# Cross-attention and sparse feed-forward on one core: the gates move from a transposed mask to an addition in the accumulators, and the probabilities' second half gets two buffers

## The chip, the cores and the metric

The kernel runs on one core of a Trainium2 chip. Its time is device time in microseconds (us), from the first to the last instruction. The engines are TensorE (PE: matmuls; PEld: its weight loads), VectorE (DVE), ScalarE (ACT), GpSimd (POOL) and SyncE (SP, which issues most DMAs). Each has its own instruction stream, and they meet in semaphores.

## The reference, cut to what matters

16 batches of 100 tokens with 1024 features (x), and 361 context rows per batch. All weights and data are float32.

```python
x = x + xattn(layernorm(x), ctx)          # 32 query heads of 128, 4 key/value heads
# q = latents @ Wq; k, v = concat(ctx, latents) @ Wk, Wv      (461 keys)
# attn = softmax(q k^T / sqrt(128)); out = (attn @ v) @ Wo
x = x + ffn(layernorm(x))
def ffn(x):                               # 1600 tokens, 3584 inner features in 56 groups of 64
    inter = x @ c1_w.T @ c2_w.T           # rank 16
    idx = argmax of inter in each group of 64
    h = relu(x . w1[idx])                 # one inner feature of each group is open
    return h @ w2t[idx]
```

## The kernel before

Products of float32 values are made of three passes: each operand is split in a high part, rounded to the fast float32 format (F32R), and a low part, the rest, and high times high, high times low and low times high are added (`PAIRS`). ACT makes the high part by a copy, DVE or POOL the low part by a subtraction.

The stages follow one another, each in a block of its own that ends when all engines have ended: keys and values, queries, attention (1195 to 2006 us in the trace), output projection, normalisation, gate weights, hidden layer (2673 to 3214 us), down projection. The change touches two.

**Attention** (`attend`). The 800 query rows of a (batch, key/value head) pair, a *group* G, are 6 tiles of 128 rows and a rest of 32; the rests of the four groups of a batch make one more tile that comes first. So a batch has 25 tiles, in steps I. In each step PE does `score(I)` (3 matmuls of 128x462), then `weigh` for tiles long done (4 matmuls, probabilities times values), then `turn(I-3)` (4 transposes of the probabilities). DVE takes the negative maximum, ACT the exponential, DVE the reciprocal of the sum, POOL scales (L1239), PE turns, ACT copies the turned tile into `pt` (L1361), DVE writes its low part (L1409). `pt` holds a whole group, 800 columns: the first 384 are weighed as half h=0, the other 416 as h=1, each in three parts in three steps. The last 32 columns of h=1 come from the rests' tile, `pt_tail`: POOL brings them in with `bring_tail(G)` (L1227). That copy stands in POOL's stream where the loop of POOL is 4 steps past tile 3 of the group, that is in the step of tile 1 of the next group, behind the scaling and behind a part of `split_q` (L1196, L1200: POOL splits the next queries in steps 0 to 2 of each group), and it first waits until the group before was weighed whole, since `pt` is the only buffer. PE's `weigh(G, 1, 0)` waits for it (`tail_in`) at L1305.

**Hidden layer** (`hidden_layer`). 1344 of the 1600 tokens (the first 256 go another way, by gathered rows that DVE multiplies and sums: `dot`, L1546, six in a pair) times all 3584 inner features. The features come in 28 blocks j of 128, two to a pair i, p = j mod 2: the first pair is written out, twelve run in PE's and ACT's loop, the last is written out. For a block PE turns the weights (`turn_w`, 2x4 transposes into the two banks `turn`), ACT and DVE split them into `w[p]` (L1749, L1779), and PE sums four tiles of 336 tokens into four banks `hid_acc` (`sums`, 24 matmuls each). The gates of a pair, 13 tiles of 128 tokens by 256 features, come in four lots of 4, 4, 4 and 1 tiles (`gates`, L1679, then `pick` on DVE: maximum, equal, times key, maximum, and L1803, the mask with 1 at the open feature). The mask has tokens on its partitions, the sums have features there. So PE turns the mask with a bf16 identity (`turn_mask`, L1691, 11 transposes a block) into the banks `turn`, once both halves of the next block's weights have left them (the wait for `low` at L1733), ACT copies it to `mask_t` (L1758), and DVE evacuates each tile with one instruction, max(sum, 0) times mask (L1827), in between its picks and dots. The order on PE is that of `body` (L1702), on DVE of L1830.

```python
                    if another:
                        pe.wait_ge(low, 2 * j + 4)
                    turn_mask(i, m, p, 0)
```

## Time and profile before

| | |
|---|---|
| time, median of 3 runs | 3652.81 us (3650.86 to 3655.02) |
| profiled execution: time, span | 3654.5 us, 3652.8 us |
| mean granted TensorE clock | 0.977 of full |
| PE busy | 3448.0 us, 94% of the span |
| DVE busy | 2295.6 us, 63% |
| ACT busy | 1369.2 us, 37% |
| POOL busy | 881.1 us, 24% |

Busy time of PE is that of modelled matmuls: the end of one lies beyond the start of the next. So what PE really lost at a place is best read from starts: where the next group of instructions starts, against where it starts when nothing is waited for. The granted clock has two levels, full (2.4 GHz) and half (1.2 GHz).

### The profile page before, as it was taken

What the parts mean: (1) busy time and instruction counts of PE and PEld (TensorE: products, weight loads), DVE (VectorE), ACT (ScalarE), POOL (GpSimd) and SP (SyncE); (2) the same over time, 40 slices, a digit from 0 to 9 for tenths busy, and PEclk for the clock granted to TensorE, in tenths of its full rate; (3) what the DMA queues carried; (4) which work ended last, traced back from release to release, by engine and by line L of the source; (5) the groups of instructions that cost most, each with busy time, mean ns of one, the idle gap of its engine ahead of it and who ended that gap; (6) DMA issues with size and microseconds to landing.
All of it is one profiled execution on the core that took longest, in us unless ns stands there. A gap on an engine that the chain in (4) does not pass through costs nothing. (4 is left out here: it accounts for less than half of the span.)

```text
span 3652.8 us, 51935 instructions
## 1 busy us (share of the span) xinstructions
PE 3448.0 (94%) x18370; PEld 3060.2 (84%) x18370; DVE 2295.6 (63%) x3858; ACT 1369.2 (37%) x2560; POOL 881.1 (24%) x1100
## 2 busy tenths in 40 slices
PE   6999999799999999999999899999789999989999
PEld 5888888799999888888888688688589999977877
DVE  5555576777765677777776433433368888766775
ACT  3333344343432776777776322322411111121120
POOL 0000000000000766676665100000001111135443
PEclk8999999899999999999999899999889999999999
DMA  3333332454443333333332644644313444488886
GB/s 125 95 101 107 101 96 79 117 139 120 118 123 106 111 109 106 107 95 102 106 107 60 198 123 120 187 119 120 115 68 132 150 151 147 147 304 313 263 289 215
DMA packets 477859, 501.44 MB, mean 137 GB/s; under 512 B 172548, under 2 KB 372228, under 8 KB 477652
## 3 DMA queue, kind: packets, MB, share of 16 engines
q1 hardware_dynamic: 441988, 371.79, 34.3%
q0 software_dynamic: 34608, 124.90, 10.1%
q8 instruction: 117, 1.92, 0.2%
q10 hardware_dynamic: 1056, 2.10, 0.2%
q14 instruction: 90, 0.74, 0.1%
HBM read 383.68 MB, written 115.02 MB: 137 GB/s over the span
## 5 line engine op out<-in xcount | busy, mean ns | idle before, releaser
L2083 PE MATMUL wo_acc<-wo_w,wo_l 128*128 128x512 f32 (+1 forms) x2496 | 576.0, 393 | 23.3 <-DVE wo_l L2033 23.3
L427 PE MATMUL kv_bank<-kv_wo,kv_so 128*128 128x512 f32 x2436 | 574.1, 395 | 16.4 <-DVE kv_wo L519 11.0
L2083 PEld LDWEIGHTS wo_acc<-wo_w,wo_l 128*128 128x128 f32 (+1 forms) x2496 | 462.5, 186 | 136.6 <-DVE wo_w L2057 25.3
L427 PEld LDWEIGHTS kv_bank<-kv_wo,kv_so 128*128 128x128 f32 x2436 | 457.6, 190 | 110.9 <-issue 17.4
L815 PE MATMUL pr_bank<-pr_xo,pr_wp 128*128 128x400 f32 x2688 | 498.8, 347 | 28.9 <-ACT pr_s L882 13.4
L815 PEld LDWEIGHTS pr_bank<-pr_xo,pr_wp 128*128 128x128 f32 x2688 | 493.6, 190 | 31.7 <-DVE pr_wp L899 24.0
L26 PE MATMUL hid_acc<-x1t,hid_w 128*128 128x336 f32 x2688 | 442.6, 323 | 1.4 <-DVE c_raw L1827 0.9
L2352 PE MATMUL w_acc<-w_w,w_l 128*128 128x512 f32 (+1 forms) x1848 | 422.0, 391 | 12.1 <-DVE w_l L2291 12.1
L26 PEld LDWEIGHTS hid_acc<-x1t,hid_w 128*128 128x128 f32 x2688 | 426.4, 194 | 2.1 <-issue 1.1
L2352 PEld LDWEIGHTS w_acc<-w_w,w_l 128*128 128x128 f32 (+1 forms) x1848 | 339.5, 184 | 94.4 <-DVE w_l L2291 12.3
L1311 PE MATMUL outs<-pt,v 128*128 128x384 f32 (+3 forms) x1536 | 347.1, 348 | 28.6 <-issue 14.4
L1409 DVE TENSOR_TENSOR pt<-turned,pt 128x512 fp32r<-128x512 f32 x384 | 264.0, 688 | 156.9 <-ACT pt L1361 153.8
L2033 DVE TENSOR_TENSOR wo_l<-wo_l_raw,wo_l 128x512 fp32r<-128x512 f32 (+1 forms) x208 | 139.3, 672 | 343.3 <-ACT wo_l L2006 343.3
L26 PE MATMUL scores<-kt,q_parts 128*128 128x462 f32 x1152 | 338.2, 402 | 3.9 <-ACT probs L1367 3.9
L1311 PEld LDWEIGHTS outs<-pt,v 128*128 128x128 f32 (+1 forms) x1536 | 277.4, 188 | 66.6 <-issue 30.7
L1239 POOL TENSOR_SCALAR probs<-probs,inverse 128x461 f32<-128x461 f32 x400 | 263.6, 659 | 250.2 <-DVE inverse L1405 249.8
L1361 ACT ACTIVATE pt<-turned 128x512 fp32r<-128x512 f32 x384 | 229.7, 598 | 169.1 <-PE turned L1292 166.0
L2006 ACT ACTIVATE wo_l<-wo_l_raw 128x512 fp32r<-128x512 f32 (+1 forms) x208 | 127.5, 615 | 404.1 <-PE wo_acc L2083 383.3
L1367 ACT ACTIVATE probs<-scores,negmax 128x461 f32<-128x461 f32 x400 | 258.0, 645 | 35.6 <-DVE negmax L1398 34.4
L1398 DVE TENSOR_REDUCE negmax<-scores 128x1 f32<-128x461 f32 x400 | 251.1, 628 | 21.4 <-PE scores L1276 21.0
L1292 PE MATMUL turned<-ident,probs 128*128 128x128 f32 x1600 | 241.1, 273 | 1.2 <-POOL probs L1239 1.2
L1292 PEld LDWEIGHTS turned<-ident,probs 128*128 128x128 f32 x1600 | 202.9, 142 | 20.0 <-POOL probs L1239 1.6
(185 smaller groups left out, 4034.8 us busy)
## 6 DMA issues: line engine op xcount, KB each, us to landing
wo_l_raw<-o_scratch SPq DMA_DIRECT2D x192, 256.0 KB, 2.9
pair_raw<-in_L_xattn_Wq_dram SPq DMA_DIRECT2D x64, 512.0 KB, 5.8
q_scratch<-pr_out SPq DMA_DIRECT2D x128, 200.0 KB, 2.4
o_scratch<-o_stage SPq DMA_DIRECT2D x64, 400.0 KB, 3.6
q_raw<-q_scratch SPq DMA_DIRECT2D x64, 384.0 KB, 3.1
stage<-in_ctx_dram SPq DMA_DIRECT2D x45, 512.0 KB, 3.9
h_scratch<-c_raw SPq DMA_DIRECT2D x28, 672.0 KB, 5.5
wo_w_raw<-in_L_xattn_Wo_dram SPq DMA_DIRECT2D x16, 1024.0 KB, 7.0
```

The source lines that it names most:

```text
L26: last = pe.matmul(out, left(a, c), right(b, c), start=(c == 0 and (a, b) == PAIRS[0]), stop=(c == chunks - 1 and (a, b) == PAIRS[-1]))
L427: last = pe.matmul(bank[:, BANK[i], :], so[:, i, a, c, :], wo[:, i, e, c, :], start=(not opened and c == 0 and (a, e) == PAIRS[0]), stop=( ...
L815: last = pe.matmul(bank[:, BANK[i], :width], wo[:, i, a, c, :], xo[:, i, e, c, :], start=(not opened and c == 0 and (a, e) == PAIRS[0]), s ...
L1239: pool.tensor_scalar(probs[:, I % RB, :kv], probs[:, I % RB, :kv], inverse[:, I % RB:I % RB + 1], 1.0, ALU.mult, ALU.mult).then_inc(scaled, 1)
L1292: last = pe.transpose(turned[:n, j % TB, k, :], probs[:, j % RB, at:at + n], ident[:, :])
L1311: last = pe.matmul(outs[:, h, :hi - lo], v[b % 2][:n, a, k, g * P:(g + 1) * P], pt[:n, e, k, lo:hi], start=(x == 0), stop=(x == NC * len(P ...
L1361: act.activation(pt_of(j, 0), turned[:, j % TB, :, :], ACT.Copy).then_inc(pt_high, 1)
L1367: act.activation(probs[:, I % RB, :kv], scores[:, I % SB, :kv], ACT.Exp, bias=negmax[:, I % RB:I % RB + 1], accum_out=total[:, I % RB:I % ...
L1398: dve.tensor_reduce(negmax[:, I % RB:I % RB + 1], scores[:, I % SB, :kv], AX.X, ALU.max, negate=True).then_inc(s_max, 1)
L1409: dve.tensor_tensor(pt_of(j, 1), turned[:, j % TB, :, :], pt_of(j, 0).bitcast(F32), ALU.subtract).then_inc(pt_low, 1)
L2083: last = pe.matmul(acc[p][:rows, :], l[j % 2][:, a, k, :rows], w[:, c, m * per + k, :], start=(m == 0 and k == 0 and (a, c) == PAIRS[0]), ...
L2352: last = pe.matmul(acc[:heights[t], n % AB, h * cols:(h + 1) * cols], l[u % LB][:, a, k, :heights[t]], w[:, b, c % slots_w, h * cols:(h + ...
```

## The change

In the hidden layer the mask is now the opposite one, 1 at every feature that is *not* open (`not_equal`). PE multiplies it, as the stationary operand, with the columns of an identity times -1e30 (`closed`, bf16) and adds the result to the sums (`close`), so a closed feature stands at about -1e30 and max(., 0) makes it 0. A tile of 336 tokens doesn't match the 128 tokens of a mask tile, so a close takes 3, 4, 3 and 4 matmuls of 16 to 128 columns, 14 a block, with 1344 columns in all, as the 11 transposes had. ACT evacuates with Relu. `turn_mask`, `mask_part`, `mask_t` and DVE's evacuations are gone. `sums` no longer ends its accumulation; `close` does and counts `summed`. The waits of PE move: for the pair's mask from behind `sums(j, p, 2)` to behind `sums(j, p, 0)`, for the next block's low parts from in front of the mask's transposes to the next block's start. On DVE the mask's last step is split off from `pick` (`mark`) and stands behind the second low part, and the dots are 2 and 4 instead of 3 and 3.

In attention `pt` becomes `pt_first` (384 columns) and two `pt_second` (416 columns each, by the group's parity). `bring_tail(G)` now comes 4 steps past tile 1, and waits for the weighing of group G-2.

```diff
-            pool.tensor_copy(ident_bf[:, :], ident[:, :]).then_inc(made, 1)
+            pool.tensor_scalar(closed[:, :], ident[:, :], -CLOSED, None, ALU.mult).then_inc(made, 1)
...
-        pt = sb("pt", [P, 2, NC, cols], F32R)
+        pt_first = sb("pt_first", [P, 2, NC, split], F32R)
+        pt_second = [sb(f"pt_second{i}", [P, 2, NC, cols - split], F32R) for i in range(2)]
...
-                if G:
-                    pool.wait_ge(o_full, 2 * G)
-                pool.tensor_copy(pt[:, :, :, body:], pt_tail[:, :, :, g * left:(g + 1) * left]).then_inc(tail_in, 1)
+                if G >= 2:
+                    pool.wait_ge(o_full, 2 * (G - 1))
+                pool.tensor_copy(pt_second[G % 2][:, :, :, body - split:],
+                                 pt_tail[:, :, :, g * left:(g + 1) * left]).then_inc(tail_in, 1)
...
-                if j >= 0 and place(j)[2] == 3:
+                if j >= 0 and place(j)[2] == 1:
                     bring_tail(place(j)[1])
...
+            def close(m, p, t):
+                for x, (k, n, a, b, lo, hi) in enumerate(parts[t]):
+                    at = k * per + p * (per // 2)
+                    last = pe.matmul(acc[:, t, lo:hi], mask[m][:n, at:at + per // 2, :].rearrange("q a b -> q (a b)"),
+                                     closed[:n, a:b], start=False, stop=(x == len(parts[t]) - 1))
+                last.then_inc(summed, 1)
...
+                    pe.wait_ge(low, 2 * j + 2)
...
                     sums(j, p, 0)
-                    if another and not early:
-                        pe.wait_ge(mask_out, 2 * j + 2)
-                        turn_w(i + p, 1 - p, 0)
+                    if p == 0:
+                        pe.wait_ge(masked, NP * (i + 1))
+                    close(m, p, 0)
+                    if another:
+                        turn_w(i + p, 1 - p, 0)
...
                     sums(j, p, 2)
-                    if another:
-                        pe.wait_ge(low, 2 * j + 4)
-                    turn_mask(i, m, p, 0)
-                    turn_mask(i, m, p, 1)
+                    close(m, p, 2)
                     if more:
-                        gates(i + 1, 0 if early else 2 * p + 1)
-                    if not early:
-                        sums(j, p, 3)
+                        gates(i + 1, 2 * p + 1)
+                    sums(j, p, 3)
+                    close(m, p, 3)
...
+            def evacuate(i, p, t):
+                j = 2 * i + p
+                act.wait_ge(summed, tiles * (j + 1) + t + 1)
+                if t == 0:
+                    act.wait_ge(stored[p], 16 * (i + 1))
+                act.activation(h[p][:, t * width:(t + 1) * width], acc[:, t, :width], ACT.Relu).then_inc(h_out, 1)
...
+                    for t in range(tiles):
+                        evacuate(i, p, t)
+                        if another and t < 2 and not (first and p == 0):
+                            high_part(j + 1, 1 - p, t)
...
-                                  ALU.is_equal).then_inc(masked, 1)
+                                  ALU.not_equal).then_inc(masked, 1)
...
-                dve.scalar_tensor_tensor(out=h[p][:, at], in0=acc[:, t, :width], scalar=0.0, in1=mask_t[:, at],
-                                         op0=ALU.max, op1=ALU.mult).then_inc(h_out, 1)
...
                     if more or p == 0:
                         low_part(j + 1, 1 - p, 1)
-                    evacuate(i, p, 0)
+                    if more and not early:
+                        mark(i + 1, 1 - m, 2 * p)
```

How the instructions stand on three engines. First PE in the hidden layer, the second block (p=1) of a pair in the loop. Before, with L1668 `turn_w`, L1679 `gates`, L26 `sums`, L1691 `turn_mask`:

```order
L26 MATMUL hid_acc<-x1t,hid_w 128x336 x24
L1666 ISA
L1668 MATMUL turn<-ident,c_raw 128x128 x4
L1676 REGISTER_ALU
L1679 MATMUL gate<-c2s,zs 128x256 x4
L1698 REGISTER_ALU
L26 MATMUL hid_acc<-x1t,hid_w 128x336 x24
L1668 MATMUL turn<-ident,c_raw 128x128 x4
L1698 REGISTER_ALU
L26 MATMUL hid_acc<-x1t,hid_w 128x336 x24
L1733 REGISTER_ALU
L1691 MATMUL turn<-ident_bf,hid_mask 128x128 x10
```

Now, with L1711 `sums`, L1702 `close`, L1682 `turn_w`, L1693 `gates`:

```order
L1711 MATMUL hid_acc<-x1t,hid_w 128x336 x24
L1702 MATMUL hid_acc<-closed,hid_mask 128x128 x2
L1702 MATMUL hid_acc<-closed,hid_mask 128x80
L1680 ISA
L1682 MATMUL turn<-ident,c_raw 128x128 x4
L1690 REGISTER_ALU
L1693 MATMUL gate<-c2s,zs 128x256 x4
L1708 REGISTER_ALU
L1711 MATMUL hid_acc<-x1t,hid_w 128x336 x24
L1702 MATMUL hid_acc<-closed,hid_mask 128x48
L1702 MATMUL hid_acc<-closed,hid_mask 128x128 x2
L1702 MATMUL hid_acc<-closed,hid_mask 128x32
```

The mask's transposes behind the third tile's sums are gone, and a close stands behind each tile's sums.

Second DVE in the same place, from the end of the third lot of gates on. Before, with L1779 the second low part, L1827 the evacuations, L1546 a dot:

```order
L1803 TENSOR_TENSOR hid_mask<-hid_equal,hid_lead 128x1024
L1779 TENSOR_TENSOR hid_w<-turn,hid_w 128x512
L1827 SCALAR_TENSOR_TENSOR c_raw<-hid_acc,hid_mask_t 128x336
L1546 ISA hid_ring,value<-hid_ring,keep 128x1024
L1546 ISA value 128x1
L1827 SCALAR_TENSOR_TENSOR c_raw<-hid_acc,hid_mask_t 128x336
L1793 TENSOR_REDUCE hid_top<-gate 128x4
L1795 TENSOR_TENSOR hid_equal<-gate,hid_top 128x256
L1797 TENSOR_TENSOR hid_equal<-hid_equal,hid_key_bf 128x256
L1801 TENSOR_REDUCE hid_lead<-hid_equal 128x4
L1803 TENSOR_TENSOR hid_mask<-hid_equal,hid_lead 128x256
L1546 ISA hid_ring,value<-hid_ring,keep 128x1024
```

Now, with L1799 the second low part, L1830 the mark, L1555 a dot:

```order
L1821 TENSOR_REDUCE hid_lead<-hid_equal 128x16
L1799 TENSOR_TENSOR hid_w<-turn,hid_w 128x512
L1830 TENSOR_TENSOR hid_mask<-hid_equal,hid_lead 128x1024
L1555 ISA hid_ring,value<-hid_ring,keep 128x1024
L1555 ISA value 128x1
L1813 TENSOR_REDUCE hid_top<-gate 128x4
L1815 TENSOR_TENSOR hid_equal<-gate,hid_top 128x256
L1817 TENSOR_TENSOR hid_equal<-hid_equal,hid_key_bf 128x256
L1821 TENSOR_REDUCE hid_lead<-hid_equal 128x4
L1830 TENSOR_TENSOR hid_mask<-hid_equal,hid_lead 128x256
L1555 ISA hid_ring,value<-hid_ring,keep 128x1024
```

The evacuations are gone, and the second low part has moved ahead of the mark.

Third POOL in attention, the third group of a batch, with L1218 (now L1224) the values' low parts. Before:

```order
L1239 TENSOR_SCALAR probs<-probs,inverse 128x461
L1218 TENSOR_TENSOR v<-v_raw,v 128x512
L1239 TENSOR_SCALAR probs<-probs,inverse 128x461
L1218 TENSOR_TENSOR v<-v_raw,v 77x512
L1239 TENSOR_SCALAR probs<-probs,inverse 128x461
L1196 TENSOR_SCALAR q_parts<-q_raw 128x384 x2
L1239 TENSOR_SCALAR probs<-probs,inverse 128x461
L1200 TENSOR_TENSOR q_parts<-q_raw,q_parts 128x384
L1227 COPY pt<-pt_tail 128x8x32
```

Now:

```order
L1247 TENSOR_SCALAR probs<-probs,inverse 128x461
L1224 TENSOR_TENSOR v<-v_raw,v 128x512
L1247 TENSOR_SCALAR probs<-probs,inverse 128x461
L1224 TENSOR_TENSOR v<-v_raw,v 77x512
L1234 COPY pt_second<-pt_tail 128x8x32
L1247 TENSOR_SCALAR probs<-probs,inverse 128x461
L1202 TENSOR_SCALAR q_parts<-q_raw 128x384 x2
L1247 TENSOR_SCALAR probs<-probs,inverse 128x461
```

The copy of the rests has moved two steps up, out of the steps with `split_q`, and here behind the values' low part.

## Rows read from the trace of the kernel before

**Rows 1.** Waits of PE, attention: engine, line <- releaser: us, times, longest.

```profile
PE outs L1311 <- issue: 14.4, 32, 0.6
PE outs L1311 <- DVE pt L1409: 14.1, 17, 0.9
```

**Rows 2.** PE timeline, attention: start, us, engine line op out<-in xcount [idle before <-releaser].

```profile
1399.01 0.88 PE L26 MATMUL scores<-kt,q_parts 128*128 128x462 f32 x3
1399.73 0.87 PE L1311 MATMUL outs<-pt,v 128*128 128x384 f32 x4
...
1400.79 0.87 PE L26 MATMUL scores<-kt,q_parts 128*128 128x462 f32 x3
1402.12 0.99 PE L1311 MATMUL outs<-pt,v 128*128 128x416 f32 x4 [0.45 <-issue]
...
1437.22 0.60 PE L1292 MATMUL turned<-ident,probs 128*128 128x128 f32 x4
1437.58 0.87 PE L26 MATMUL scores<-kt,q_parts 128*128 128x462 f32 x3
1439.34 0.99 PE L1311 MATMUL outs<-pt,v 128*128 128x416 f32 x4 [0.89 <-DVE pt L1409]
```

**Rows 3.** Timeline of POOL, the same stretch.

```profile
1401.62 0.40 POOL L1227 CAST pt<-pt_tail 128x256 fp32r<-128x256 f32 x1
...
1435.66 0.67 POOL L1239 TENSOR_SCALAR probs<-probs,inverse 128x461 f32<-128x461 f32 x1
...
1438.83 0.40 POOL L1227 CAST pt<-pt_tail 128x256 fp32r<-128x256 f32 x1
```

**Rows 4.** Windows, hidden layer: stretch, length, PE, PEld, DVE, ACT, POOL busy, clock, DMA.

```profile
2731.28:3182.33 451.05, 425.87 (x2918) 416.40 (x2916) 375.77 (x549) 61.21 (x96) 81.00 (x71) 0.98 0.41 145
2835.60:2839.00 3.40, 3.40 (x18) 3.14 (x16) 1.50 (x2) 1.35 (x2) 0.00 (x0) 0.50 0.02 6
```

**Rows 5.** Timeline of PE, hidden layer, one pair.

```profile
2862.70 0.60 PE L1668 MATMUL turn<-ident,c_raw 128*128 128x128 f32 x4
...
2863.61 3.85 PE L26 MATMUL hid_acc<-x1t,hid_w 128*128 128x336 f32 x24
2867.31 0.60 PE L1668 MATMUL turn<-ident,c_raw 128*128 128x128 f32 x4
2867.66 3.93 PE L26 MATMUL hid_acc<-x1t,hid_w 128*128 128x336 f32 x24
2873.69 0.86 PE L1691 MATMUL turn<-ident_bf,hid_mask 128*128 128x128 bf16 x11 [2.10 <-DVE hid_w L1779]
2874.49 0.39 PE L1679 MATMUL gate<-c2s,zs 80*128 x1
...
2887.10 3.93 PE L26 MATMUL hid_acc<-x1t,hid_w 128*128 128x336 f32 x24
2890.88 0.87 PE L1691 MATMUL turn<-ident_bf,hid_mask 128*128 128x128 bf16 x11
...
2899.69 0.60 PE L1668 MATMUL turn<-ident,c_raw 128*128 128x128 f32 x4
```

**Rows 6.** Waits of PE, hidden layer.

```profile
PE turn L1691 <- DVE hid_w L1779: 30.7, 14, 3.9
```

**Rows 7.** Timeline of DVE, the same pair.

```profile
2866.73 0.68 DVE L1779 TENSOR_TENSOR hid_w<-turn,hid_w 128x512 fp32r<-128x512 f32 x1
...
2872.95 0.68 DVE L1779 TENSOR_TENSOR hid_w<-turn,hid_w 128x512 fp32r<-128x512 f32 x1
...
2877.78 0.42 DVE L1793 TENSOR_REDUCE hid_top<-gate 128x4 f32<-128x256 f32 x1
...
2879.81 1.22 DVE L1546 CUSTOM_DVE_ANT_0 hid_ring<-hid_ring,keep 128x1024 f32<-128x1024 f32 x1
```

**Rows 8.** Timeline of PE, first pair's end and second's start.

```profile
2721.86 9.58 PE L26 MATMUL hid_acc<-x1t,hid_w 128*128 128x336 f32 x48
2731.28 0.60 PE L1668 MATMUL turn<-ident,hid_raw 128*128 128x128 f32 x4
```

More of the change, by code:

```diff
@@ L1573, in hidden_layer @@
     NP = len(picks)
-    parts = ((sparse.S, 8), (sparse.S + 8, tt - 8 - sparse.S))
+    parts = [[] for _ in range(tiles)]
+    for k in range(sparse.S, tt):
+        at, n = k * P - skip, P if k < tt - 1 else tail
+        for t in range(tiles):
+            lo, hi = max(at, t * width), min(at + n, (t + 1) * width)
+            if lo < hi:
+                parts[t].append((k, n, lo - at, hi - at, lo - t * width, hi - t * width))
     landed, turned = [sem(f"w1_landed{i}") for i in range(2)], sem("w1_turned")
@@ L1682, in gates @@
                 last.then_inc(gated, 1)
-            def turn_mask(i, m, p, s):
-                lo, n = parts[s]
-                if p == 0 and s == 0:
-                    pe.wait_ge(masked, NP * (i + 1))
-                for k in range(n):
-                    q = P if lo + k < tt - 1 else tail
-                    at = (lo + k) * per + p * (per // 2)
-                    last = pe.transpose(turn[:, s, :].bitcast(BF16)[:, k * P:k * P + q],
-                                        mask[m][:q, at:at + per // 2, :].rearrange("q a b -> q (a b)"),
-                                        ident_bf[:q, :q])
-                last.then_inc(mask_turned, 1)
+            def close(m, p, t):
[4 more added lines that the diff above has]
+                last.then_inc(summed, 1)
             def sums(j, p, t):
                 pe.wait_ge(h_out, tiles * j + t + 1)
-                product(pe, acc[:, t, :width], lambda a, c: w[p][:, a, c, :],
-                        lambda a, c: x1t[:, a, c, skip + t * width:skip + (t + 1) * width], chunks).then_inc(summed, 1)
+                for c in range(chunks):
+                    for a, b in PAIRS:
+                        pe.matmul(acc[:, t, :width], w[p][:, a, c, :],
+                                  x1t[:, b, c, skip + t * width:skip + (t + 1) * width],
+                                  start=(c == 0 and (a, b) == PAIRS[0]), stop=False)
             def body(i, m, more, first):
@@ L1707, in body @@
                     late = first and p == 1
+                    pe.wait_ge(low, 2 * j + 2)
                     if early:
-                        gates(0, 0)
-                    pe.wait_ge(low, 2 * j + 2)
-                    sums(j, p, 0)
-                    if early or late:
-                        gates(1 if late else 0, 1)
-                    if another and not early:
-                        pe.wait_ge(mask_out, 2 * j + 2)
+                        for t in range(tiles):
+                            gates(0, t)
+                            sums(j, p, t)
+                        turn_w(0, 1, 0)
+                        turn_w(0, 1, 1)
+                        pe.wait_ge(masked, NP)
+                        for t in range(tiles):
+                            close(m, p, t)
+                        gates(1, 0)
+                        continue
+                    sums(j, p, 0)
+                    if p == 0:
+                        pe.wait_ge(masked, NP * (i + 1))
+                    close(m, p, 0)
+                    if late:
+                        gates(1, 1)
+                    if another:
                         turn_w(i + p, 1 - p, 0)
@@ L1720, in body @@
                     sums(j, p, 1)
[L1721 to L1723 removed]
+                    close(m, p, 1)
+                    if late:
+                        gates(1, 2)
+                    if another:
                         turn_w(i + p, 1 - p, 1)
                     sums(j, p, 2)
[L1726 to L1735 removed]
+                    close(m, p, 2)
                     if more:
[L1737 to L1739 removed]
+                        gates(i + 1, 2 * p + 1)
+                    sums(j, p, 3)
+                    close(m, p, 3)
             turn_w(0, 0, 0)
@@ L1762, in body @@
                     j = 2 * i + p
-                    if more or p == 0:
+                    another = more or p == 0
+                    if another:
                         act.wait_ge(summed, tiles * (j + 1))
+                    if another and first and p == 0:
                         high_part(j + 1, 1 - p, 0)
                         high_part(j + 1, 1 - p, 1)
-                    mask_part(j, 0)
-                    mask_part(j, 1)
+                    for t in range(tiles):
+                        evacuate(i, p, t)
+                        if another and t < 2 and not (first and p == 0):
+                            high_part(j + 1, 1 - p, t)
             high_part(0, 0, 0)
@@ L1834, in body @@
                     late = first and p == 1
-                    dots = [] if first else [sparse.PER_PAIR * (i - 1) + sparse.PER_PAIR // 2 * p + n
-                                             for n in range(sparse.PER_PAIR // 2)]
+                    at = sparse.PER_PAIR * (i - 1)
+                    dots = [] if first else list(range(at, at + 2) if p == 0 else range(at + 2, at + sparse.PER_PAIR))
                     if early:
@@ L1839, in body @@
                             pick(0, 0, k)
+                            mark(0, 0, k)
                             if k == 0:
```

63 lines of the change are left out of this document (24 added, 39 removed).

## Prediction

> **What bounds the kernel now.** First the busy shares of the page: PE works 94% of the span (the table above), so only what PE waits for, and what it does, can move the end. Then the waits of PE in the two stages that the change touches, and the timeline of PE at these waits, read from starts.
>
> In attention PE waits at one line, `weigh`: 32 waits of 14.4 us in all without a named releaser and 17 of 14.1 us put down to DVE [rows 1]. Usually a `weigh` starts 0.72 us after the scores before it (1399.73 - 1399.01); where its first matmul is that of half h=1 it starts 1.33 us after (1402.12) or 1.76 us after (1439.34) [rows 2]. So the true losses are 0.61 and 1.04 us, where the column of idle time shows 0.45 and 0.89: it leaves out 0.16 us, hidden by the modelled end of the scores. Total: 28.5 + 49 x 0.16 = 36.3 us. The releaser is neither "issue" nor DVE: POOL's copy of the rests starts at 1401.62 and takes 0.40 us, PE starts at 1402.12; it starts at 1438.83, PE starts at 1439.34 [rows 3]. Twice the start comes 0.1 us after its end.
>
> In the hidden layer twelve pairs take 451.05 us, 37.59 us each, with DVE busy for 375.77 us, 31.3 us a pair [rows 4]. A pair without a slow stretch takes 2899.69 - 2862.70 = 36.99 us [rows 5]. PE waits once in a pair, ahead of the mask's transposes of p=1, for DVE's second low part: 14 waits, 30.7 us by the idle column, the longest 3.9 us [rows 6]. By starts the one in [rows 5] is longer: sums to mask take 3.78 us where nothing is waited for (2890.88 - 2887.10), so 2873.69 - 2867.66 - 3.78 = 2.25 us. Why DVE is late: the first low part begins at 2866.73, a whole pick with its mask stands between, and the second begins at 2872.95 [rows 7].
>
> Behind some of these waits the granted clock is 0.50 (1.2 GHz) for 3.4 us [rows 4]. The mean pair is 37.59 - 36.99 = 0.60 us longer than the undisturbed one; that is the clock's share, 7.2 us in twelve pairs.
>
> **The change, part by part.**
>
> *Attention.* The copy moves two steps up. A step is 1.78 us (1400.79 - 1399.01 [rows 2]), so the copy comes some 3.5 us sooner, where it is now late by 1.04 us at most. Its new wait, for group G-2, is met long before. Its instruction (0.40 us) still costs POOL the same. What is late next: in the third group it now stands behind a low part of V and ahead of the scaling at 1435.66. That scaling ends at 1436.33 and PE turns its tile at 1437.22 [rows 2, 3], 0.9 us later; 0.4 us of it go, 0.5 us remain. The other input of that `weigh`, DVE's low part of tile 5, is also needed by the transposes right behind, which show no wait today. Gain: 36.3 us less what scheduling leaves, 35.5 us. Bounds: 37 us (the small delays below the idle column go too), and 18 us, half, if POOL's later scalings take over some of the waits.
>
> *Hidden layer, what goes.* The wait of 2.25 us and the clock's share leave 36.99 - 2.25 = 34.74 us a pair. The mask's transposes go: 11 take 0.80 us (2874.49 - 2873.69), and the change of kind before them costs 0.08 us (3.78 us against 3.70 us = 2867.31 - 2863.61 for the same 24 sums) [rows 5]; twice a pair that is 1.76 us. Left: 32.98 us.
>
> *What is added.* 28 closes a pair, bf16 with 128 stationary columns as the transposes. Price by count: 0.80/11 = 0.073 us, 2.04 us a pair. Price by moving columns: the same 1344 a block, so 1.60 us. Upper bound, the price of a float32 matmul of the sums, 3.70/24 = 0.154 us: 4.3 us. I take the count, since loads as many as matmuls are the likelier limit of such small pieces. Eight changes of kind, 0.08 us each: 0.64 us. A pair: 32.98 + 2.04 + 0.64 = 35.66 us, 1.93 us less than 37.59; twelve pairs give 23.2 us (the bounds: 36 us with columns and no cost of changing, a loss of 4 us with 0.154 us).
>
> On the price of a close the Trainium skill speaks against the change: "TensorE: Matmul & The Clock Gate", section on LDWEIGHTS, has a load cost its columns over 1.2 GHz, whatever the rows, so some 0.107 us for a close of any width, an estimate by that page; the sum would then be 36.6 us a pair. The trace speaks against the figure for bf16, since 11 transposes with such loads took 0.80 us, but it bears out that pieces of few columns need not be cheap.
>
> *DVE* loses eight evacuations a pair of 336 columns, each below the 0.68 us of a low part of 512 [rows 7], so its load falls from 31.3 us towards 26 to 28 us in 35.7. Is it in time? The second low part is now wanted at the next block's start. The last mark of a pair is wanted 3.7 us into the next pair, behind its first sums, where before it had the time of two sums more. In the block p=1 DVE needs a low part, a big pick and a mark (2872.95 - 2866.73 = 6.2 us), another low part 0.7, a dot 1.2, and the small pick with mark 2.0 (2879.81 - 2877.78) [rows 7]: 10.1 us. It can start about 5.3 us into the block (sums, close, four transposes, ACT's copy), so it ends at 15.4 us; PE wants it at 17.8 + 3.7 = 21.5 us. 6 us are to spare. The second low part ends at about 11 us, wanted at 17.8.
>
> *ACT* takes eight evacuations and loses four mask copies; it is busy 61.21 us of 451.05 [rows 4], so 5 us a pair, and will have about 6. High parts stand behind an evacuation of half a microsecond each; that is in the 5.3 us above.
>
> *First and last pair.* In the first the mask wait of 3.9 us [rows 6] goes, and with it the slow clock behind it: 48 sums took 2731.28 - 2721.86 = 9.4 us where 7.4 are due [rows 8], 2.0 us. Against that the first gates now wait for the first low parts. Net 6 us (3 to 9). The last pair has no such wait today and pays (2.04 + 0.64 - 1.76)/2 = 0.46 us a block: 1 us lost.
>
> Sum: 35.5 + 23.2 + 6 - 1 = 63.7 us, from the span of 3652.8 us: 3589 us. The profiled run took 3654.5 us, 1.7 us above its span, and the median is 3652.81, so the span can stand for the median. Predicted 3588 us.
>
> **Rivals.**
> - *Dear closes.* Each is held by its load or by adding into a bank just written. At 0.11 us, midway between 0.073 and 0.154: 32.98 + 3.08 + 0.64 = 36.7 us a pair, 10.7 us instead of 23.2, and 2 us more in the outer pairs: 3603 us; at 0.154 us 3620 us. For it: 14 pieces instead of 11, and small ones; against: the transposes' 0.073. 12%. The Trainium skill's rule on LDWEIGHTS, above, gives nearly the first of these prices.
> - *Attention's wait passes on.* With 0.5 us to spare at the third group, POOL's scalings make `turn` wait; half the gain is left, 3606 us. For it: that narrow place; against: it is one in four groups. 10%.
> - *The copy was not the releaser.* Then DVE, as 17 waits say, and attention gains nothing: 3624 us. Against: 0.1 us from the copy's end to PE's start, twice. 4%.
> - *Slower.* Closes don't overlap: each matmul of `close` waits until the one before has drained into the bank. The price is the length of a lone matmul, 0.39 us (the single one of gates at 2874.49 [rows 5]). A pair takes 32.98 + 0.64 + 28 x 0.39 = 44.5 us, 6.9 more than today; twelve lose 83 us, the outer pairs 13 more after what the first gains, attention gives back 35.5: 3713 us. It decides from 12 x (28x - 3.97) + 2 x (28x - 1.12) = 42.5, x = 0.23 us a close. Against it: sums add to one bank in a row at 0.154 us. 3%.
>
> **How the numbers follow.** The forecast has 71%, its own range 3573 to 3599. For 8 in 10 the range takes the first two rivals nearly whole: 3569 to 3611 us. Faster by over 0.2% (7 us, about what a measurement of this kernel can tell) 96%, within 0.2% 1%, slower 3%.
>
> **What would show it.** Right: no waits of PE at `weigh`, POOL's copy two steps ahead; a period of 35.7 us in the hidden layer, PE waiting nowhere in it and its clock at 1.0 in the loop, 14 closes at 1.0 us a block; DVE with idle time before the low parts. Wrong: PE waiting at `close` for the last mark, at `turn` in attention for POOL, or closes above 0.1 us.

## The result, and the profile after

| | before | after |
|---|---|---|
| time, median of 4 runs | 3652.70 us (3650.86 to 3655.02) | 3571.61 us (3570.39 to 3572.71) |
| span of the profiled execution | 3652.8 us | 3570.2 us |
| mean granted TensorE clock | 0.977 | 0.981 |
| attention, first to last `weigh` | 798.4 us | 757.1 us |
| hidden layer, first pair | 58.6 us | 48.8 us |
| hidden layer, twelve looped pairs | 451.05 us | 421.20 us |
| hidden layer's last pair to the down projection's first matmul | 40.8 us | 39.0 us |

The change makes the kernel faster: the ratio is 0.9778, 95% interval 0.9761 to 0.9795, 81.1 us. The prediction was 3588 us in a range of 3569 to 3611. The sign and the range held, near the range's lower edge and just outside the forecast's own 3573 to 3599; the gain was underestimated by 19 us of span. The stages say where: attention gave 41.4 us (counted: 35.5), the loop 29.9 (23.2), the first pair 9.8 (6), the last pair with what follows it 1.8 (-1).

The busy line of the page after:

```profile
PE 3425.1 (96%) x18454; PEld 3049.2 (85%) x18454; DVE 2249.9 (63%) x3746; ACT 1379.7 (39%) x2616; POOL 868.4 (24%) x1100
```

Waits of PE in attention (us in total, times, longest). The 49 of [rows 1] are two:

```profile
PE turned L1300 <- POOL probs L1247: 1.1, 1, 1.1
PE outs L1319 <- DVE pt_second L1418: 0.7, 1, 0.7
PE outs L1319 <- DVE pt_first L1418: 0.2, 1, 0.2
```

Timelines of PE and POOL there (start, us, engine, line, operation), at the first part of a half h=1:

```profile
1486.08 0.88 PE L27 MATMUL scores<-kt,q_parts 128*128 128x462 f32 x3
1486.80 0.92 PE L1319 MATMUL outs<-pt_second,v 128*128 128x416 f32 x4
1487.55 0.60 PE L1300 MATMUL turned<-ident,probs 128*128 128x128 f32 x4
...
1481.26 0.40 POOL L1234 CAST pt_second<-pt_tail 128x256 fp32r<-128x256 f32 x1
```

`weigh` starts 0.72 us after the scores, as where nothing is waited for, instead of 1.33 or 1.76 [rows 2]. POOL's copy is done 5.1 us before PE needs it; before it was done 0.1 us before PE started [rows 3].

In the hidden layer the wait of [rows 6], 14 times in 30.7 us, is gone; what PE waits for is at its start and in the first pair. The window of the twelve looped pairs (columns as in [rows 4]) has PE busy throughout and the clock at 1.00:

```profile
PE turn L1682 <- DMA c_raw<-in_L_ffn_w_dram: 5.0, 1, 5.0
PE gate L1693 <- DVE hid_w L1799: 1.5, 1, 1.5
...
2680.12:3101.32 421.20, 421.20 (x2992) 406.46 (x2990) 336.76 (x456) 71.26 (x144) 70.51 (x72) 1.00 0.45 155
```

PE in a block p=1 of the loop, and DVE in the same block:

```profile
2802.99 0.32 PE L1702 MATMUL hid_acc<-closed,hid_mask 128*128 128x128 bf16 x3
2803.15 0.63 PE L1682 MATMUL turn<-ident,c_raw 128*128 128x128 f32 x4
...
2804.09 3.85 PE L1711 MATMUL hid_acc<-x1t,hid_w 128*128 128x336 f32 x24
2807.78 0.33 PE L1702 MATMUL hid_acc<-closed,hid_mask 128*128 128x48 bf16 x4
2807.96 0.63 PE L1682 MATMUL turn<-ident,c_raw 128*128 128x128 f32 x4
2808.35 3.93 PE L1711 MATMUL hid_acc<-x1t,hid_w 128*128 128x336 f32 x24
2812.12 0.32 PE L1702 MATMUL hid_acc<-closed,hid_mask 128*128 128x96 bf16 x3
2812.26 0.36 PE L1693 MATMUL gate<-c2s,zs 80*128 x1
2812.46 3.90 PE L1711 MATMUL hid_acc<-x1t,hid_w 128*128 128x336 f32 x24
2816.20 0.44 PE L1702 MATMUL hid_acc<-closed,hid_mask 128*128 128x16 bf16 x4
2816.58 3.95 PE L1711 MATMUL hid_acc<-x1t,hid_w 128*128 128x336 f32 x24
2820.37 0.32 PE L1702 MATMUL hid_acc<-closed,hid_mask 128*128 128x128 bf16 x3
```

```profile
2804.45 0.69 DVE L1799 TENSOR_TENSOR hid_w<-turn,hid_w 128x512 fp32r<-128x512 f32 x1 [2.28 <-ACT hid_w L1765]
...
2814.36 0.42 DVE L1830 TENSOR_TENSOR hid_mask<-hid_equal,hid_lead 128x256 bf16<-128x256 bf16 x1
...
2821.82 0.69 DVE L1799 TENSOR_TENSOR hid_w<-turn,hid_w 128x512 fp32r<-128x512 f32 x1 [3.39 <-ACT hid_w L1765]
```

From start to next start, a block's four closes take 0.16, 0.18, 0.14 and 0.38 us. The sums before them take 3.69, 3.77, 3.74 and 3.79 us, where 3.70 was the length without a change of kind. DVE now waits 2.28 us before the first low part of p=1, which it came late for before [rows 7], and 3.39 us before that of the next block; the last mark is there at 2814.78 and wanted at 2820.37, 5.6 us later.

### The profile page after: what moved, and what is told of

The parts are those of the page before. It is cut to its first block and busy times, and to the rows that moved or that the text cites. A ratio compares the mean times of both kernels' runs of the same rounds, so it can differ in the third digit from the quotient of the medians.

```text
span 3570.2 us, 52022 instructions
## 1 busy us (share of the span) xinstructions
PE 3425.1 (96%) x18454; PEld 3049.2 (85%) x18454; DVE 2249.9 (63%) x3746; ACT 1379.7 (39%) x2616; POOL 868.4 (24%) x1100
## 3 DMA queue, kind: packets, MB, share of 16 engines
q1 hardware_dynamic: 441988, 371.79, 35.5%
## 5 line engine op out<-in xcount | busy, mean ns | idle before, releaser
L1711 PE MATMUL hid_acc<-x1t,hid_w 128*128 128x336 f32 x2688 | 440.0, 319 | 0.0
L1711 PEld LDWEIGHTS hid_acc<-x1t,hid_w 128*128 128x128 f32 x2688 | 415.6, 189 | 1.1
L1774 ACT ACTIVATE c_raw<-hid_acc 128x336 f32<-128x336 f32 x112 | 50.2, 452 | 392.1 <-PE hid_acc L1702 392.1
L27 PEld LDWEIGHTS scores<-kt,q_parts 128*128 128x128 f32 x1152 | 189.4, 191 | 13.0 <-ACT probs L1376 4.3
L1418 DVE TENSOR_TENSOR pt_first<-turned,pt_first 128x512 fp32r<-128x512 f32 x192 | 132.2, 689 | 86.2 <-ACT pt_first L1370 85.0
L1548 POOL DMA_INDIRECT w_ring<-in_L_ffn_w2t_dram,idx x112 | 143.9, 1285 | 171.0 <-DVE w_ys L1563 53.2
```

Source lines behind the costliest of these rows:

```text
L27: last = pe.matmul(out, left(a, c), right(b, c), start=(c == 0 and (a, b) == PAIRS[0]), stop=(c == chunks - 1 and (a, b) == PAIRS[-1]))
L1548: return pool.indirect_dma_start(row[:, :], None, (self.w1 if kind == "in" else self.w2t)[:, :], bass.IndirectOffsetOnAxis(self.idx[:, s, ...
L1711: pe.matmul(acc[:, t, :width], w[p][:, a, c, :], x1t[:, b, c, skip + t * width:skip + (t + 1) * width], start=(c == 0 and (a, b) == PAIRS[ ...
```

## The experiments

All times are medians; each ratio is against the kernel before on the same chip. Its medians were 3651.53 us (the first four kernels), 3649.72 (`close_twice`, `full_rows`, `full_gates`, `low_back`) and 3649.47 (the other four), against 3652.70 beside the change. So whole times of different chips compare to some 3 us only, and small effects are read from the stages. "Looped pairs" is the length of the twelve pairs, read as in the table.

### Each half alone

`att_only` has the attention edit alone, `hid_only` the hidden layer's alone.

> The kernel before with attention alone changed (two buffers for the second half, the copy of the rests two steps up). My theory: attention is 41 us shorter, 36 us of waits of PE for POOL's copy and 5 us of weight loads that stood bare behind each wait, and nothing else moves: 3612 us. Rival, the two edits lean on each other (DMA traffic or the clock of a later stage changes with the earlier one): more than 4 us away from that.

> The changed kernel with the attention of before, so that only the hidden layer is changed. My theory: the hidden layer is 41 us shorter (10 in the first pair, 30 in the twelve, 2 in the last), 3612 us, with a pair at 35.1 us and the granted clock at 1.0 in its loop. Rival, the stages lean on each other: more than 4 us away.

Measured: `att_only` 3607.73 us, ratio 0.9886 (0.9869 to 0.9902), attention 757.07 us, looped pairs 451.05. `hid_only` 3612.07 us, 0.9895 (0.9879 to 0.9912), attention 798.40, looped pairs 421.19. The two gains, 43.8 and 39.5 us, add up to 83.3 where the change has 81.1, within what the intervals allow, and each stage alone is as long as in the change (757.07 and 421.20 us): the halves don't touch each other.

### Attention: the place or the second buffer

`two_late` keeps the two buffers, with the copy at its old place:

```diff
-                if j >= 0 and place(j)[2] == 1:
+                if j >= 0 and place(j)[2] == 3:
                     bring_tail(place(j)[1])
```

> The changed kernel with POOL's copy of the rests back at its old place, 4 steps past tile 3, but with the two buffers kept. My theory, the place of the copy makes the gain, the buffers only allow it: attention takes what it took before, 3613 us. Rival, the single buffer and its wait for the group before held the copy back: 3572 us, as the changed kernel.

`one_ahead` is the kernel before with its single buffer; the copy only moves within its step, from the step's end to behind the scaling, ahead of `split_q` and of the values' low parts:

```diff
+                j = I - LAG - 1
+                if j >= 0 and place(j)[2] == 3:
+                    bring_tail(place(j)[1])
+                if I < N:
                     if t is not None and t < 3 and G + 1 < NGR:
...
-                j = I - LAG - 1
-                if j >= 0 and place(j)[2] == 3:
-                    bring_tail(place(j)[1])
```

> The kernel before, one buffer, with the copy of the rests still in the step of tile 3 plus 4, but ahead of the split of the next queries in that step and no longer behind it, so 1.0 us sooner. My theory, the copy is what PE waits for, by 0.6, 0.15, 0.6 and 1.04 us in a batch's four groups: nearly all waits go, 3613 to 3617 us. Rival, DVE's low part releases PE, as the trace puts down 17 of the 49 waits: no change, 3653 us.

Measured: `two_late` 3613.61 us, 0.9893 (0.9876 to 0.9909), attention 797.75 us, no gain left in it. `one_ahead` 3610.19 us, 0.9885 (0.9869 to 0.9902), attention 758.83 us. The waits of PE at `weigh`, of `two_late` first, then of `one_ahead`:

```profile
PE outs L1319 <- issue: 13.9, 32, 0.6
PE outs L1319 <- DVE pt_first L1418: 13.1, 16, 0.9
```

```profile
PE outs L1312 <- DVE pt L1410: 0.9, 2, 0.7
```

So POOL's copy was the releaser of the 49 waits (two of 0.9 us in all are left), though the trace put 17 of them down to DVE: `one_ahead` touches nothing but POOL's order. The place makes the gain. The earlier place that the second buffer allows brings 1.8 us more.

### The price of a close

`close_twice` adds every close a second time (28 more pieces a pair; a closed feature is still closed):

```diff
-                for x, (k, n, a, b, lo, hi) in enumerate(parts[t]):
+                twice = parts[t] + parts[t]
+                for x, (k, n, a, b, lo, hi) in enumerate(twice):
```

> The changed kernel with every close done twice (-2e30 instead of -1e30, the same gates), 28 more small matmuls a pair and 392 in all. Price by columns, 2688 columns more a pair at 1/2.4 ns each = 1.1 us, 16 us in 14 pairs, and up to 6 us more if each piece with 64 rows costs 0.2 us: 3587 to 3593 us. Rival, my prediction's price by count, 0.073 us: 29 us, 3600 us. Rival, closes that wait for the one before to drain, 0.2 us and more: 3650 us.

`full_rows` is about the fourth tile's last piece. 1344 tokens are 10 mask tiles of 128 rows and one of 64, so this piece alone works on 64 rows. Here it takes all 128 (the identity is zero in the added rows, so the sums are the same):

```diff
-        at, n = k * P - skip, P if k < tt - 1 else tail
+        at, n, rows = k * P - skip, P if k < tt - 1 else tail, P
...
-                parts[t].append((k, n, lo - at, hi - at, lo - t * width, hi - t * width))
+                parts[t].append((k, rows, lo - at, hi - at, lo - t * width, hi - t * width))
```

> The changed kernel, but the close's piece for the last mask tile, which has 64 tokens, is given all 128 rows (the identity has zeros in the rows past 64, so the sums are the same). In the changed kernel the fourth close is 0.37 us long, to the next sums, where the second with as many pieces takes 0.18. My theory, the piece with 64 rows makes the next load or matmul stand bare: the fourth close falls to about 0.18 us, 28 times 0.2 = 5.5 us, 3566 us. Rival, the fourth close is long because the next block begins with waits and register arithmetic: no change, 3571 us.

Measured: `close_twice` 3592.14 us, 0.9845 (0.9830 to 0.9860); looped pairs 441.60 us, 36.80 each, 1.70 us more for 28 pieces. `full_rows` 3563.01 us, 0.9767 (0.9753 to 0.9780); looped pairs 416.00 us, 34.67 each. Its median is 8.6 us below the change's, but the edit didn't make all of that: its hidden layer begins 3.5 us sooner (2627.83 against 2631.28 us), and its ratio overlaps with the change's. What the edit gives is read in the loop, 5.2 us. The fourth close on PE's timeline, of `close_twice` first, then of `full_rows`:

```profile
2819.60 0.82 PE L1703 MATMUL hid_acc<-closed,hid_mask 128*128 128x16 bf16 x8
2820.35 1.81 PE L1712 MATMUL hid_acc<-x1t,hid_w 128*128 128x336 f32 x10
```

```profile
2811.08 0.34 PE L1702 MATMUL hid_acc<-closed,hid_mask 128*128 128x16 bf16 x4
2811.25 3.93 PE L1711 MATMUL hid_acc<-x1t,hid_w 128*128 128x336 f32 x24
```

Doubled, the first three closes take 0.31, 0.34 and 0.29 us from start to next start, 0.15, 0.16 and 0.15 us more: ten full-row pieces for 0.46 us, 0.046 us each, which goes by their 1008 columns (0.42 us at 2.4 GHz), not by their number. The fourth takes 0.37 us more, to 0.75. With 128 rows it falls from 0.38 to 0.17 us. So the one piece with 64 rows costs some 0.2 us each time, with its load, and twice that when it comes twice. Twenty-four of them are in the loop, 5.2 us.

The trace shows where the 0.2 us sit: in the start of two weight loads. The change's fourth close, from its third piece on, then the load behind the last piece in `full_rows`:

```profile
2816.30 0.35 PE L1702 MATMUL hid_acc<-closed,hid_mask 128*128 128x128 bf16 x2
...
2816.44 0.09 PEld L1702 LDWEIGHTS hid_acc<-closed,hid_mask 64*128 64x128 bf16 x1
...
2816.57 0.19 PEld L1711 LDWEIGHTS hid_acc<-x1t,hid_w 128*128 128x128 f32 x1
```

```profile
2811.23 0.19 PEld L1711 LDWEIGHTS hid_acc<-x1t,hid_w 128*128 128x128 f32 x1
```

The load of 64 rows starts 0.14 us behind the start of the third piece, and the load behind it 0.12 us behind the start of the last (2816.45). In `full_rows` the third and the last piece start at 2811.17 and 2811.22, and the loads behind them in the same hundredth or the next. So one load before and one behind the odd piece lose their overlap, 0.1 us each. Fewer rows alone don't do it: the gates' first load, of 80 rows, starts at 2803.51 behind a turning of 128 rows that starts at 2803.50. Why 64 rows do is not shown.

### Where the loop's wait went

The prediction has DVE's second low part come late because a pick stands in front of it. The change did four things about that: PE waits for it later, DVE does it sooner, DVE has no evacuations, and no mask goes through the transposes. These kernels put them back one after another. `low_back` has PE's wait at its old place:

```diff
                     sums(j, p, 2)
                     close(m, p, 2)
+                    if another:
+                        pe.wait_ge(low, 2 * j + 4)
```

> The changed kernel with PE's wait for the next block's low parts put back behind the third tile (before the gates there), where the kernel before had it and lost 2.2 us a pair. Theory, DVE's relief alone makes the low parts early enough (the second ends some 2 us before that place): no change, 3572 us. Rival, the wait went because it was moved: about 25 us slower, with PE waiting there for DVE.

`order_back` has that too, and DVE's old order (mark ahead of the second low part, dots 3 and 3):

```diff
                     if more and not early:
                         pick(i + 1, 1 - m, 2 * p)
-                    if more or p == 0:
-                        low_part(j + 1, 1 - p, 1)
-                    if more and not early:
                         mark(i + 1, 1 - m, 2 * p)
                         if p == 0:
                             indices(i + 1)
+                    if more or p == 0:
+                        low_part(j + 1, 1 - p, 1)
```

> The changed kernel with DVE's order of before (mark at once behind its pick and ahead of the second low part, three dots in each block) and PE's wait for the low parts back behind the third tile. Only the evacuations are still off DVE. Theory: the second low part comes 1.2 us later than in the changed kernel, where 2.1 us are to spare, so PE waits nowhere in the loop: 3572 us. Rival, the new order is needed: about 1 us a pair and more, 3585 us.

`evac_back` has DVE's old order and its evacuations (max(sum, 0) without the mask, which is in the sums already), and PE's wait in the new place; `evac_back_low` has PE's wait in the old place as well. Both have this:

```diff
+            def evacuate(i, p, t):
+                j = 2 * i + p
+                dve.wait_ge(summed, tiles * (j + 1) + t + 1)
+                if t == 0:
+                    dve.wait_ge(stored[p], 16 * (i + 1))
+                dve.tensor_scalar(h[p][:, t * width:(t + 1) * width], acc[:, t, :width], 0.0, None,
+                                  ALU.max).then_inc(h_out, 1)
```

> As order_back, but PE's wait stays at the next block's start as in the changed kernel, and the evacuations are DVE's again (max with 0), at their places of before. Theory: the second low part, 10.9 us behind the block's first weight transposes as in the kernel before, is wanted 17.4 us behind them, so the low parts cost nothing; the last mark comes 17.2 us behind them, about when the first close of the next pair wants it: 0 to 0.5 us a pair, 3572 to 3579 us. So moving the wait alone would do. Rival, DVE's relief is needed: 3590 us or more.

> As evac_back, and PE's wait back behind the third tile, wanted 9.1 us behind the block's first weight transposes: DVE and the wait as in the kernel before, only closes instead of transposes and copies. Theory: the wait of before returns, 1.9 us in each of 12 pairs, with slow stretches of the clock behind some of them (3 to 7 us): 3598 to 3604 us. Rival, the wait came of the mask's way over the banks of the turned weights and not of DVE: 3572 us.

| | median | ratio (95%) | looped pairs | first pair |
|---|---|---|---|---|
| the change | 3571.61 us | 0.9778 (0.9761 to 0.9795) | 421.20 us | 48.84 us |
| `low_back` | 3572.10 | 0.9791 (0.9776 to 0.9806) | 421.20 | 52.38 |
| `order_back` | 3576.36 | 0.9795 (0.9779 to 0.9811) | 421.20 | 55.61 |
| `evac_back` | 3571.24 | 0.9783 (0.9767 to 0.9799) | 421.20 | 50.37 |
| `evac_back_low` | 3577.51 | 0.9803 (0.9787 to 0.9819) | 421.20 | 56.11 |

`evac_back_low` missed its expectation (3598 to 3604 us) and went to its rival's side: with all of DVE's old work and order, and PE's wait in its old place, the wait does not come back in the loop. Its window shows DVE as busy as before (375.77 us, [rows 4]), and PE busy throughout:

```profile
2685.65:3106.85 421.20, 421.20 (x2992) 406.47 (x2990) 375.62 (x552) 28.80 (x48) 83.29 (x72) 1.00 0.44 155
```

What differs from before is what DVE waits for. In the kernel before, its first evacuation of a block waited for ACT's copy of the turned mask, which waits for PE's transposes of the mask. ACT's copy, DVE's first evacuation in each block of a pair, and the next second low part that PE waits for:

```profile
2874.35 1.35 ACT L1758 ACTIVATE hid_mask_t<-turn 128x1024 bf16<-128x1024 bf16 x2 [5.81 <-PE turn L1691]
...
2875.79 0.51 DVE L1827 SCALAR_TENSOR_TENSOR c_raw<-hid_acc,hid_mask_t 128x336 f32<-128x336 f32 x1 [2.16 <-issue]
...
2892.98 0.51 DVE L1827 SCALAR_TENSOR_TENSOR c_raw<-hid_acc,hid_mask_t 128x336 f32<-128x336 f32 x1 [2.57 <-issue]
...
2909.94 0.68 DVE L1779 TENSOR_TENSOR hid_w<-turn,hid_w 128x512 fp32r<-128x512 f32 x1
```

In `evac_back_low` DVE (first and second low part) and PE (the wanted place, behind the third close):

```profile
2809.97 0.69 DVE L1800 TENSOR_TENSOR hid_w<-turn,hid_w 128x512 fp32r<-128x512 f32 x1
...
2816.20 0.69 DVE L1800 TENSOR_TENSOR hid_w<-turn,hid_w 128x512 fp32r<-128x512 f32 x1
```

```profile
2808.68 0.63 PE L1682 MATMUL turn<-ident,c_raw 128*128 128x128 f32 x4
...
2817.78 0.36 PE L1693 MATMUL gate<-c2s,zs 80*128 x1
```

Without the mask's route DVE begins the first low part of p=1 2809.97 - 2808.68 = 1.29 us after PE's turning, with the same amount of work in the same order, where it began 2866.73 - 2862.70 = 4.03 us after [rows 5, 7]. The second one ends at 2816.89, 0.9 us before PE wants it.

Of DVE's two idle times the one in p=0 made the wait. From the evacuation at 2892.98 to the second low part of the next p=1 at 2909.94 DVE has no idle time in the trace, and that low part ends at 2910.62. PE wants it where its sums are done: they start at 2904.65, and 3.78 us later is 2908.43. Without the 2.57 us of standing the low part would be done at 2908.05, an estimate from these rows, just in time. So the wait came down a chain: PE turned the mask of p=0 behind its third tile, ACT copied it, DVE stood for the copy and then had 17 us of work up to the low part. The 2.16 us in p=1 come behind PE's wait and are made good, since DVE waits again for the next block's first low part (0.32 us at 2883.41, and in every pair).

Taking the mask's route away was enough in the loop; moving the wait, the order and the evacuations was not needed. In the first pair, where all starts late, they count: putting back PE's wait costs 3.5 us, with DVE's order 6.8 (`order_back` was expected at 3572 us and missed it by this), with all of it 7.3. There PE waits, and the clock is low behind it, as in `order_back`:

```profile
2675.57 0.55 PE L1693 MATMUL gate<-c2s,zs 80*128 80x256 f32 x1 [4.79 <-DVE hid_w L1801]
2675.92 6.41 PE L1711 MATMUL hid_acc<-x1t,hid_w 128*128 128x336 f32 x24
```

### How much DVE can take

`dve_load8` adds eight reductions over 1024 elements to each looped pair, on DVE ahead of the last small pick and its mark:

```diff
+                    if p == 1 and more and not first:
+                        for n in range(LOAD):
+                            dve.tensor_reduce(extra[:, LOAD * i + n:LOAD * i + n + 1], sparse.keep[0][:, :],
+                                              AX.X, ALU.max)
```

> The changed kernel with 8 more reductions on DVE (128x1024 float32 to one column, some 1.2 us each) ahead of the last pick of each of 12 pairs, 9.6 us a pair. Their results are used by nothing. By the trace DVE waits for 6.5 us in a pair, and the last mark has 5.6 us to spare. Theory: PE waits for the last mark in each pair, and the period becomes DVE's, 35.1 - 6.5 + 9.6 = 38.2 us: 37 us more and up to 7 us of slow clock, 3609 to 3616 us. Rival, DVE has more room than its idle time shows, the period stays below 37 us: under 3595 us.

Measured: 3637.06 us, ratio 0.9962 (0.9948 to 0.9977); looped pairs 487.45 us, 40.62 each, clock 0.971 over the run. PE around the mark, then the added work:

```profile
2788.37 3.95 PE L1713 MATMUL hid_acc<-x1t,hid_w 128*128 128x336 f32 x24
2795.28 0.46 PE L1704 MATMUL hid_acc<-closed,hid_mask 128*128 128x128 bf16 x3 [2.96 <-DVE hid_mask L1832]
...
2802.75 0.33 PE L1704 MATMUL hid_acc<-closed,hid_mask 128*128 128x48 bf16 x4
```

```profile
2784.09 9.10 DVE L1878 TENSOR_REDUCE hid_extra<-keep 128x1 f32<-128x1024 f32 x8
```

The added 9.1 us exceed the 5.6 us of slack by 3.5; PE waits 2795.28 - 2788.37 - 3.79 = 3.12 us, so the slack that the prediction counted on is real. The price was larger than expected because each such wait lowers the clock: close, turning, gates and sums take 2802.75 - 2795.28 = 7.47 us behind it, where the change takes 4.79 (2825.16 - 2820.37 of its next block), 2.7 us more. The first of the twelve pays less: the pairs' lengths are 38.22, 39.85, 40.85 and then 40.9 to 41.0 us. On average a pair pays 5.5 us for a wait of 3.1, and the expectation (3609 to 3616 us) missed by that. The change's margin is thus the thing to keep: 5.6 us of DVE time a pair. With 3.5 us beyond it the loop lost 66 us, more than twice its gain.

### One step further

`full_gates` is `full_rows` with the first gates of the first pair ahead of the wait for the first low parts:

```diff
+                    if early:
+                        gates(0, 0)
...
-                            gates(0, t)
+                            if t:
+                                gates(0, t)
```

> As full_rows, and the first gates of the hidden layer stand ahead of the wait for the first low parts again, as in the kernel before. Theory: 1.5 us of the wait before the first gates go and with them up to 1 us of DVE's start, 3564 us. Rival: the first pair waits for DVE's four picks anyway and the start is set by DVE's low parts, 0 to 1 us, as full_rows.

Measured: 3561.72 us, ratio 0.9759 (0.9746 to 0.9772), the first pair 46.84 us instead of 48.69 in `full_rows`, looped pairs 416.00. It is the fastest version of the study by median and span (3557.6 us); against `full_rows` the intervals overlap, and the 1.85 us in the first pair are what the trace shows of it.

## Why the prediction was right, and where it was short

**What bounds the kernel: right.** PE's waits in the two stages were what there was to gain, and reading them from starts gave their size. That POOL's copy, not "issue" or DVE, released `weigh` was the reading with the most at stake (36 us); `two_late` and `one_ahead` settle it.

**Attention: mechanism right, 6 us short (41.4 for 35.5).** The term counted the delay of the first matmul only. The parts behind a wait were also longer: 1402.95 - 1402.12 = 0.83 us from `weigh` to the transposes in the kernel before, 1487.55 - 1486.80 = 0.75 us now, with the same four matmuls. The first weight load has no matmul to hide behind after a wait. By starts over the whole stage the way from scores to `weigh` is 37.3 us shorter (58 parts were late by more than 0.13 us; the idle column has 49) and that from `weigh` to the transposes 4.0 us. So of the 5.9 us missing 4.0 are bare loads, 1.0 are waits too short for the idle column or cut by it, and 0.8 the sum had held back. That POOL's scalings would take over the waits (10%) is excluded: one wait of 1.1 us for POOL stands in the stage, and the kernel before had it too (1.2 us).

**The close: the count was the wrong of two prices.** The working had 0.073 us a piece and 0.64 us a pair for changes of kind, 2.68 us. The rows give 2 x 0.86 us for closes and 2 x 0.20 us for the changes, 2.1 us. The other price named, by columns (1.60 us), was nearer to the 1.72 us, and it was left out for a reason that doesn't hold: loads as many as matmuls don't limit such pieces, since `close_twice` added full-row pieces at 0.046 us. The eleven transposes' 0.80 us held a 64-row tile too, and the trace of before tells them apart: ten full-row ones start 0.056 us apart, and the tile of 64 rows takes 0.15 us ahead of it and 0.13 us behind it (2891.39, 2891.55 and 2891.68 us). A pair has two such odd tiles, in the transposes' price as in the closes' 1.72 us. Against the Trainium skill ("TensorE: Matmul & The Clock Gate", section on LDWEIGHTS: a load costs its columns over 1.2 GHz and nothing by its rows) `close_twice` is plain: added full-row pieces with 128-column loads cost 0.046 us each, less than half of the page's figure. With the page's word on rows the trace agrees for the load itself, 0.09 us with 64 rows and 0.10 with 128; what the 64 rows changed is when loads start. The page's price would have given 36.6 us a pair; the trace has 35.10.

**The wait in the hidden layer: right that it goes, wrong why; its term came out by luck.** The sum took out 2.25 + 0.60 us a pair, and 37.59 - 35.10 = 2.49 us, with 0.36 us added by masks and closes (2.12 - 1.76), gives 2.85: the same number. So the size of the wait was read rightly; that this change would end it was luck. The argument went by DVE's load and by where the low part is wanted. `evac_back_low` shows that neither was needed. The step that was missing is what DVE itself waited for: 2.57 us ahead of the evacuations of p=0, without a named releaser, on an engine read only for its busy time. Had the change kept the mask's route and moved the rest, this argument would have promised the same gain; that version was not run, so whether the other three moves would have been enough by themselves stays open.

**First pair: 9.8 us, not 6.** The wait of 3.9 us and the slow sums of [rows 8] went, as counted, and the first gates now wait 1.5 us, where the first sums waited 0.56 us. What was left out is that this pair had a second slow stretch. Before, first block's end; after, the same sums:

```profile
2698.05 0.86 PE L1691 MATMUL turn<-ident_bf,hid_mask 128*128 128x128 bf16 x11 [1.64 <-DVE hid_w L1779]
...
2700.81 6.21 PE L26 MATMUL hid_acc<-x1t,hid_w 128*128 128x336 f32 x24 [0.87 <-DVE c_raw L1827]
```

```profile
2657.11 3.95 PE L1711 MATMUL hid_acc<-x1t,hid_w 128*128 128x336 f32 x24
```

Two waits, 2.5 us, and 2.3 us of clock went with the transposes and with DVE's evacuations.

**Last pair: 1.8 us gained, not 1 lost.** PE's own work did grow, but by 0.2 us (28.74 to 28.91 us from the start of the pair to the end of its sums). The gap to the down projection shrank from 12.05 to 10.06 us. DVE's last evacuation, then PE's first matmul of the next stage, before; then ACT's last and PE's first after:

```profile
3213.06 0.50 DVE L1827 SCALAR_TENSOR_TENSOR c_raw<-hid_acc,hid_mask_t 128x336 f32<-128x336 f32 x1
...
3223.13 3.33 PE L2352 MATMUL w_acc<-w_w,w_l 128*128 128x512 f32 x7 [12.05 <-DVE w_l L2291]
```

```profile
3130.27 0.45 ACT L1774 ACTIVATE c_raw<-hid_acc 128x336 f32<-128x336 f32 x1 [3.63 <-PE hid_acc L1702]
...
3140.29 2.05 PE L2367 MATMUL w_acc<-w_w,w_l 128*128 128x512 f32 x4 [10.06 <-DVE w_l L2306]
```

DVE could begin the last block's four evacuations only at 3208.37, behind ACT's copy of the turned mask, and had dots in between, so two of them came after PE's end (3211.07). The last bank was out 2.5 us after that end, and is out 0.5 us after it with ACT. The prediction priced PE there and not the way out of the stage.

**The rivals.** Dear closes, closes that don't overlap (0.23 us each from which the change would lose) and the copy not being the releaser are all refuted by the numbers above.

## What to carry to other kernels

Before an operation is moved from one engine to another, follow the wait back along its chain: not only whom the bounding engine waits for, but whom that one waits for, and read its idle time without a named releaser as closely as its busy time. A queue's order can be worth as much as a buffer: one copy moved ahead of its neighbours on an engine that is 24% busy gave 40 us. Price small matmuls by their columns where they have full rows, look at the odd piece at the end by itself, and add to every wait of TensorE removed the bare load behind it and the clock that it costs.

## What the runs showed of the hardware

- A bf16 matmul of 64 rows between others of 128 costs some 0.2 us where the same piece with 128 rows, half of them of no use, costs none of it: 0.38 us against 0.17 for the close, 5.2 us in twelve pairs. Its own weight load and the one behind it start 0.14 and 0.12 us behind the start of the matmul before, where full-row loads start within 0.01 us of it. A load of 80 rows behind a matmul of 128 starts within 0.01 us too.
- A mask as the stationary operand, with an identity as the moving one, adds into a bank behind float32 sums at the speed of its columns: 0.14 to 0.18 us for 336 columns, with a changed kind costing at most 0.09 us.
- A weight load behind a wait, with nothing to hide it, adds 0.08 us (0.83 against 0.75 us for the same four matmuls).
- The granted clock fell around waits of about 3.1 us in each looped pair of `dve_load8`, and cost 2.7 us for each from the second on, nearly as much as the wait itself. In the kernel before, with waits of 2.25 us, it fell in five of twelve pairs ([rows 4] has one at 0.50), which took 38.4 us instead of 36.99.
